# When the shared expert's weights are loaded, and in what order the expert routing is worked out, in a two-layer decoder on one core

## The reference

```python
logits = x @ w_router.T
_, top_idx = jax.lax.top_k(logits, TOP_K)            # TOP_K = 1
mask = jax.nn.one_hot(top_idx, E, dtype=logits.dtype).sum(axis=1)
scores = jax.nn.sigmoid(logits) * mask
masked_inputs = scores.T[:, :, None] * x[None, :, :]
gate_up = jnp.einsum('eth,ehf->etf', masked_inputs, gate_up_proj)
gate, up = jnp.split(gate_up, 2, axis=-1)
expert_out = jnp.einsum('etf,efh->eth', up * jax.nn.silu(gate), down_proj)
shared = jax.nn.silu(x @ w_gate.T) * (x @ w_up.T) @ w_down.T
out = shared + expert_out.sum(axis=0)
```

## Time and profile before

| | |
|---|---|
| median of three runs | 1583.07 us |
| the profiled execution | 1582.05 us |
| its span | 1580.3 us |
| PE busy | 1408.4 us (89%) |
| DVE busy | 1085.4 us (69%) |
| ACT busy | 742.1 us (47%) |
| POOL busy | 334.6 us (21%) |
| mean granted clock of PE | 0.94 of full speed |

### The profile page before, as it was taken

The page is one execution under the profiler, slowest core; times in us unless marked ns, Lnnn a source line. Parts: engine busy times, 40 slices in busy tenths (PEclk is TensorE's granted clock), DMA queues, the critical chain, the costliest instruction groups (busy, mean ns, idle before and its releaser), DMA issues. The chain is left out here.

```text
span 1580.3 us, 24782 instructions
## 1 busy us (share of the span) xinstructions
PE 1408.4 (89%) x9358; PEld 758.7 (48%) x9358; DVE 1085.4 (69%) x2384; ACT 742.1 (47%) x995; POOL 334.6 (21%) x393
## 2 busy tenths in 40 slices
PE   6876699968999979868998889999999999999976
PEld 3544478844989876422334512333333333332555
DVE  3899655542221217866984789999999999994447
ACT  2444344421111111324664315777778777778431
POOL 3323210013000017742334520000000000000241
PEclk9998899979999999858999968999999999999998
DMA  9644600025889841673430650342223422220001
GB/s 345 222 146 146 187 1 1 1 87 208 290 280 304 276 148 53 192 214 118 130 91 15 185 178 1 83 101 67 64 64 86 101 65 64 64 63 2 1 1 53
DMA packets 148745, 185.57 MB, mean 117 GB/s; under 512 B 15723, under 2 KB 124799, under 8 KB 148498
## 3 DMA queue, kind: packets, MB, share of 16 engines
q1 hardware_dynamic: 135836, 150.65, 31.7%
q0 software_dynamic: 9200, 29.64, 6.0%
q10 hardware_dynamic: 3590, 3.70, 0.7%
HBM read 129.52 MB, written 54.15 MB: 116 GB/s over the span
## 5 line engine op out<-in xcount | busy, mean ns | idle before, releaser
L1934 DVE TENSOR_REDUCE xa_part<-psum 128x1 f32<-128x512 f32 x768 | 481.6, 683 | 25.9 <-PE psum L1795 24.9
L1894 ACT ACTIVATE xa_P<-psum 128x1024 f32<-128x1024 f32 (+1 forms) x416 | 403.2, 1021 | 139.0 <-PE psum L1819 137.7
L1819 PE MATMUL psum<-sa_Q,xa_K 50*128 50x512 bf16 (+3 forms) x1664 | 262.9, 380 | 4.6 <-DMA sa_Q<-xa_mrow 3.6
L1795 PE MATMUL psum<-xa_K,sa_Q 48*128 48x512 bf16 x768 | 241.0, 397 | 6.0 <-DVE xa_part L1934 4.5
L1835 PE MATMUL psum<-xa_P,xa_V 128*32 128x512 f32 (+1 forms) x1664 | 222.5, 607 | 0.4 <-ACT xa_P L1894 0.4
L1795 PEld LDWEIGHTS psum<-xa_K,sa_Q 48*128 48x128 bf16 x768 | 59.1, 93 | 234.8 <-DVE xa_part L1934 203.5
L1931 DVE CUSTOM_DVE_ANT_0 psum<-psum,cf_sb 128x128 f32<-128x128 f32 (+3 forms) x256 | 119.5, 517 | 32.4 <-PE psum L1795 32.2
L1819 PEld LDWEIGHTS psum<-sa_Q,xa_K 50*128 50x128 bf16 (+3 forms) x1664 | 102.5, 96 | 76.9 <-ACT xa_P L1894 20.9
L1187 PEld LDWEIGHTS psum<-xtT,wgu 128*128 128x128 f32 x992 | 115.5, 192 | 5.8 <-issue 4.6
L1187 PE MATMUL psum<-xtT,wgu 128*128 128x128 f32 x992 | 115.9, 275 | 1.4 <-issue 0.8
L1894 ACT ACTIVATE sa_P<-psum 128x1024 f32<-128x1024 f32 (+3 forms) x128 | 83.5, 707 | 57.0 <-PE psum L1819 56.8
(11 more groups left out here) (241 smaller groups left out, 2170.5 us busy)
## 6 DMA issues: line engine op xcount, KB each, us to landing
wgu<-in_f_gu SPq DMA_DIRECT2D x31, 1024.0 KB, 6.2
xa_K<-kx SPq DMA_DIRECT2D x192, 100.1 KB, 5.1
wdn<-in_f_dn SPq DMA_DIRECT2D x31, 512.0 KB, 6.6
vx<-xv_v SPq DMA_DIRECT2D x48, 256.0 KB, 3.8
xa_V<-vx POOLq DMA_DIRECT2D x16, 768.0 KB, 6.5
sa_Q<-qs SPq DMA_DIRECT2D x64, 96.0 KB, 2.3
sa_K<-ks SPq DMA_DIRECT2D x64, 96.0 KB, 2.3
sa_Q<-qx SPq DMA_DIRECT2D x64, 96.0 KB, 2.3
```

The costliest lines, as they stand in the source:

```text
L1795: last = pe.matmul(out[:, 0:width], hb.q(u)[tile:tile + HALF, to, qt * P:(qt + 1) * P], hb.k(u)[tile:tile + HALF, to, e * BANK:e * BANK + ...
L1819: last = pe.matmul(out(j), hb.k(u)[tile:tile + depth, to, kt * P:kt * P + r], hb.q(u)[tile:tile + depth, to, q0(kt):L], start=(half == 0), ...
L1894: act.activation(Pr[0:r, (u * KT + kt) % PR, h:h + 2, 0:w_], S_PS(p)[0:r, :, 0:w_], ACT.Exp, scale=SCALE).then_inc(s_exp, 1)
L1934: dve.tensor_reduce(part[:, g % 2, col + qt, e:e + 1], src, AX, ALU.max).then_inc(s_1free, 1)
```

## The change

It has four parts.

1. The three loads of list "f" are issued by SP in `l0_xattn`, behind the context's loads, and no longer by ACT in `l0_ffn`. Their semaphore f_w is made there. The weights lie in a region of their own, `big_weights`, allocated for the whole program ahead of layer 0; layer 1's last weights (list "d") take the same region later.
2. On PE, the rank matmuls stand between the gate half and the up half of item 1, instead of behind item 1.
3. On DVE, the order behind the counts becomes: clearing cs, the sigmoid, item 0's product, the steps to the tile ends, the table, item 1's product, the slots; then, ahead of the products of items 2, 3, 4 and 5, four scalings each.
4. In `combine_and_prepare` the tiles of `Values` are allocated ahead of those of `Split`, and in `heads_loop` ACT gets one more wait, `keys.val.sp_end(act)`, for all stores of the values, ahead of its first exponential.

```diff
--- before.py
+++ after.py
@@ -801,6 +801,7 @@
+        env.s_fw = sem("f_w")
@@ -814,6 +815,8 @@
+                for dst, src in env.loads["f"]:
+                    sp.dma_start(dst, src).then_inc(env.s_fw, 16)
@@ -1055,20 +1057,22 @@
-        def shared_pe(pe, n):
+        def shared_pe(pe, n, halves=range(2)):
             c, f = items[n]
             if n == 0:
-                pe.wait_ge(s_fw, 16 * len(env.loads["f"]))
+                pe.wait_ge(env.s_fw, 16 * len(env.loads["f"]))
...
-            for e, name in enumerate(("f_wg", "f_wu")):
+            for e in halves:
+                name = ("f_wg", "f_wu")[e]
...
-            last.then_inc(s_sps, 1)
+            if e == 1:
+                last.then_inc(s_sps, 1)
@@ -1198,12 +1202,13 @@
-                    for n in range(2):
-                        shared_pe(pe, n)
+                    shared_pe(pe, 0)
+                    shared_pe(pe, 1, (0,))
                     pe.wait_ge(s_cnt, 1)
                     pe.matmul(PS[:, BANK:BANK + E], env.tri, pre[:, T, :], start=True, stop=True)
                     pe.matmul(PS[:, BANK + E:BANK + 2 * E], env.ones, pre[:, T, :], start=True,
                               stop=True).then_inc(s_rank, 1)
+                    shared_pe(pe, 1, (1,))
@@ -1232,8 +1237,6 @@
-                    for dst, src in env.loads["f"]:
-                        act.dma_start(dst, src).then_inc(s_fw, 16)
@@ -1293,14 +1296,11 @@
                     ins.then_inc(s_cnt, 1)
-                    shared_dve(dve, 0)
+                    link(dve.memset(cs[:, :, :], 0.0))
                     dve.wait_ge(s_ex, 1)
                     link(dve.tensor_scalar(e1[:, :], en[:, :], 1.0, None, ALU.add))
                     link(dve.reciprocal(sg[:, :], e1[:, :]))
-                    for t in range(T):
-                        dve.tensor_scalar(xs[:, t, :], env.x[:, t, :], sg[:, t:t + 1], None, ALU.mult).then_inc(s_xs, 1)
-                    shared_dve(dve, 1)
-                    link(dve.memset(cs[:, :, :], 0.0))
+                    shared_dve(dve, 0)
                     dve.wait_ge(s_rank, 1)
@@ -1311,18 +1311,21 @@
                     end = cs[:, 0, E:2 * E]
+                    link(dve.tensor_tensor(le[:, :, :], end[0:1, :].unsqueeze(1).to_broadcast([1, ETILES, E]),
+                                           iota32[0:1, :].unsqueeze(2).to_broadcast([1, ETILES, E]), ALU.is_le))
+                    link(dve.tensor_reduce(tf[:, :], le[:, :, :], AX, ALU.add))
+                    link(dve.tensor_scalar(tf2[:, :], tf[:, :], float(E - 1), None, ALU.min))
+                    dve.tensor_copy(table[:, :], tf2[:, :]).then_inc(s_tab, 1)
+                    shared_dve(dve, 1)
                     link(dve.tensor_tensor(st[:, :], end, nt[:, :], ALU.subtract))
...
                     dve.tensor_copy(slot[:, :], sf[:, :]).then_inc(s_slot, 1)
...
                     for n in range(2, ROUTE_ITEMS):
+                        for t in range((n - 2) * TB, min((n - 1) * TB, T)):
+                            dve.tensor_scalar(xs[:, t, :], env.x[:, t, :], sg[:, t:t + 1], None, ALU.mult).then_inc(s_xs, 1)
                         shared_dve(dve, n)
@@ -1381,9 +1384,9 @@
+        val = Values(env, c_, "sv", [(b, tuple(range(TB)), P) for b in range(B)], env.vs)
         sp_ = Split(env, c_, "sqk", L, bias, dst, lambda n: [(part,) for part in SLOTS[blocks[n][1]]], 4,
                     rope=lambda n: (env.cos, env.sin_neg if blocks[n][2] == 0 else env.sin))
-        val = Values(env, c_, "sv", [(b, tuple(range(TB)), P) for b in range(B)], env.vs)
@@ -1904,6 +1907,7 @@
                     act.wait_ge(keys.split.s_lo, keys.rest[-1] + 1)
+                    keys.val.sp_end(act)
@@ -2367,6 +2377,8 @@
+        big = sb("big_weights", [P, 3 * KD * F], F32)
+        weights("f", ctx, big)
@@ -2388,10 +2400,8 @@
-        with ExitStack() as c0:
-            weights("f", c0)
-            later_keys = l0_ffn(nc, env, sa)
-        weights("d", ctx)
+        later_keys = l0_ffn(nc, env, sa)
+        weights("d", ctx, big)
```

More of the change, by code:

```diff
@@ L1031, in l0_ffn @@
         s_l1 = sem("f_l1")
-        s_fw = sem("f_w")
         s_dve = sem("f_dve")
@@ L2341, in build, with weights @@
         env.w, env.loads = {}, {"a": [], "c": [], "f": [], "1": [], "d": []}
-        def weights(layer, c):
+        def weights(layer, c, region=None):
             sbw, _ = alloc(c)
+            used = 0
             for name, (k, n, l) in MATS.items():
@@ L2351, in weights @@
                     else:
-                        t = sbw(name + "_sb", [P, k // P, n], F32)
+                        if region is None:
+                            t = sbw(name + "_sb", [P, k // P, n], F32)
+                        else:
+                            t = region[:, used:used + k // P * n].rearrange("p (k n) -> p k n", n=n)
+                            used += k // P * n
                         env.w[name] = t
```

## The result

| | before | after |
|---|---|---|
| median | 1582.88 us (8 runs, 1574.33 to 1587.16) | 1568.84 us (8 runs, 1562.37 to 1574.76) |
| the profiled execution | 1582.05 us | 1574.76 us |
| its span | 1580.3 us | 1573.0 us |

The ratio is 0.991, with a 95% interval of 0.9889 to 0.9932. The sign and what bounds the block were right; three terms of the sum were not. Three executions in all the measurements (1831.3, 2025.97 and 3388.97 us) were far slower than the rest and count in no median or ratio here.

The account below looks back on a forecast made before the run. Bound: TensorE's expert tiles, started late by the shared items and scatters behind late weights. First turn 10.8 us sooner, less 2.0 for the clock, gives 8.8: 1573.25 us profiled, forecast 1574.3; range 1569.8 to 1579.5.

Parts of the forecast that it names:

- what bounds the block: Feed-forward block: TensorE-bound expert tiles from 386.5 to 577 us; whatever starts them sooner is passed on whole.
- the sum: Whole kernel: 10.8 us gained at the first turn, less 2.0 for the clock, 8.8 us.
- both chains: Ahead of the expert tiles: ten shared items and the scatters end last at about the same time; both must move.
- the load costs nothing: SP's queue in the stage before: SP has nothing else to issue, engines move 1 GB/s; 135 us to spare.
- the new wait is covered: Layer 1 self attention: ACT's 2.9 to 4.0 us delay fits in PE's 5.93 us idle time, 1.9 us to spare.
- the lock: DVE scalings beside POOL scatters: the engines hold each other up; 2.0 us taken, between nothing and 4.3.
- the clock: PE behind the first turn: after idling some 4 us it starts at the lower clock, costing 2.0 us.
- the landing: Last scatter to row loads: kept as before, within the 25.03 us from first scatter to first turn.
- rival 2: Scatters and items: the lock costs in full, 2.8 us for the clock; 5.2 gained, 1577.9 us; chance 0.14.
- rival 1: Scatters: the lock costs nothing, slots at 346.5; 13.3 us gained less 1.65, 1571.4 us; chance 0.16.

Follow-up runs that it names:

- the kernel with the wait later: Changed kernel with ScalarE's new wait moved behind the first four exponentials of the heads: median 1570.14 us, ratio 0.9919 to before.
- the burst of 16: Changed kernel with all 16 scalings straight behind the slots instead of four ahead of each of four products: median 1569.1 us, ratio 0.9895 to before.
- layout only: Kernel before with only the new allocations and ACT's new wait, old load place and orders: median 1582.75 us, ratio 0.9975.
- loads only: Changed kernel with DVE's and PE's orders of before, keeping the early loads and their allocations: median 1572.09 us, ratio 0.993 to before.
- the late rank: Changed kernel with the rank matmuls behind the whole of item 1 again: median 1571.24 us, ratio 0.9913 to before.
- the eleventh item: Changed kernel with eleven instead of ten shared items ahead of the expert tiles: median 1566.99 us, ratio 0.9907 to before.

## Why the prediction was right, and where it was too small

**Right: what bounds the block, and that both chains move.** PE waits neither for weights nor for hT, and the last thing to be late is the chain of scatters. The first turn was forecast at 374.7 with a block start at 332.54, that is +42.2; the profile has +38.9.

**Right: the load costs nothing.** SP issued the three loads at 200.2 to 201.6 us, and the stage that they run in (from its first matmul to the feed-forward block) took 148.0 and 150.5 us in the change's two profiles, 148.2 and 150.6 in before's.

**Right: the new wait is covered**, to a tenth of a microsecond against before (+33.8 against +33.9) and to 0.4 against the kernel with the wait later, and its delay of 4.1 us was within 0.1 of the upper bound.

**Wrong in size: the sum.** Six terms, counted from the block's start, in microseconds gained against the prediction:

| term | predicted | measured | gained |
|---|---|---|---|
| slots ready | +14.46 | +14.02 | 0.44 |
| slots to first scatter | 0.64 | 1.11 | -0.47 |
| first to last scatter, with the lock | 19.31 + 2.0 | 19.19 | 2.12 |
| last scatter to row loads | 3.69, as before | 2.41 | 1.28 |
| row loads to turn | 2.03 | 2.16 | -0.13 |
| the clock behind the turn | 2.0 | 0 (1.6 in the second profile) | 2.0 |

Their sum is 5.2 us, and 8.8 + 5.2 = 14.0. What failed are three terms that were sized too high: the lock (2.0, measured 0), the landing (3.69, measured 2.41) and the clock (2.0, measured 0 or 1.6). Each is a step of the text:

- "I take 2.0" for the lock. The two engines do hold each other up: the rows at 613 pointed to it, and the burst of 16 shows it. What failed is the step from one blocked instruction to a price for sixteen. I let each burst hit POOL; in fact the first burst is over when the first scatter starts, and beside the second and third it is one scaling of DVE's that waits, 0.1 to 0.2 us each, while the scatters keep their pace. The rule of the Trainium skill (SBUF — State Buffer, Who interferes with whom) is that whoever starts first keeps the pair for the whole instruction and the other blocks. The trace agrees with it only in part: the scatter in the burst of 16 waits, and a scaling that reaches the end of a scatter waits for that end, but scalings that began up to 0.45 us into a scatter ran at their usual 0.34 us. The rule names no total; the order of the two engines' instructions had to be walked through one by one, and rival 2 was priced without that.
- "As before" for the landing. I let the 25.03 us from first scatter to turn stand, as if the DMA engines were as full as before. In before the table came last, so the first experts' 4.5 MB were still moving when the last scatter was issued; with the table first they are done by then. The windows from the last scatter to the row loads, in before and then in after (DMA share and GB/s are the last two numbers):

```profile
379.80:383.50 3.70, 3.70 (x10) 1.55 (x9) 0.69 (x1) 0.60 (x1) 0.93 (x1) 1.00 0.61 228
```

```profile
375.10:377.50 2.40, 2.40 (x7) 0.94 (x5) 0.64 (x1) 0.00 (x0) 0.93 (x1) 1.00 0.31 109
```

  The experiments divide cleanly by this: with the table last (before twice, layout only, loads only) it is 3.7 to 4.6 us, with the table first (all the others, the one with the late rank and the one with the burst among them) 2.4. That the moving weights are the reason is read from the windows; no run changes the traffic alone. "The 18 us by which the table comes sooner are worth nothing by themselves" was therefore wrong by 1.3 us.
- "I take 2.0" for the clock. I reckoned with 4 us of idling; it was 1.8, since the turn came 3.3 us sooner than thought. The price was about right where the clock does fall (1.6 to 2.5 us). It did so in one of the change's two profiles, so how much of this term the medians hold is not known.

**The range.** All three errors were in one direction, and rival 1, which had the lock at nothing, kept the other two terms. Its 1571.4 with 1.3 us less for the landing and 1.65 less for the clock would have been 1568.4. The low end had 1.6 us beyond rival 1, not enough for the landing and the clock together.

**What stays open.** The total moved by 14.0 us in the medians, as much as the turn did. That the first stages add nothing is the likeliest reading of fourteen block starts that lie between 332.4 and 340.8 us with either layout; a difference of 1 or 2 us in their mean can't be excluded with these runs. The stages behind the first gather took 984 to 993 us in these profiles, so they too hide such a difference. Open as well: what delays ACT's silu ahead of the turn in some executions, and what lets the clock fall behind one stop of 1.8 us and not behind another.

## What to carry to other kernels

Where the parts of a change lie on one chain, they add up at the end of that chain: 10.9 and 3.0 us apart, 14.1 together. Read them there; further on, one fall of the clock (2.8 us in the loads-only profile) looks like an interaction. Moving a step that starts large loads ahead of a stream of small DMAs can shorten the landing of the stream's last transfer, even if nobody waits for those loads: 2.4 us here instead of 3.7. And when an engine idles for a transfer right ahead of a long run of matmuls, work from the run itself can fill the gap: the eleventh item gave 1.7 us at the first gather for one changed number.

## What the runs showed of the hardware

- VectorE and GpSimd hold each other up, and who waits depends on the moment. A DMA_INDIRECT that began 1.2 us into 16 back-to-back scalings took 3.21 us instead of 1.10 and ended 0.12 us behind the last of them; the 16 took the same 4.29 us as with GpSimd idle. Beside shorter bursts only the end of a DMA_INDIRECT of 0.96 us holds VectorE up: scalings that began up to 0.45 us into it took their usual 0.34 us, those that began 0.51 to 0.72 us into it ended 0.09 us behind its end. One that began 0.08 us into a burst of four took its usual 0.96 us.
- The first scatter starts 0.3 us behind the slots if its data has long been there, and 1.1 us behind them (0.85 us behind the end of the first scaling) if the scalings come after the slots.
- A stop of 1.8 us let the granted clock fall to 0.50 in one execution and not in another of the same program, and the 32 matmuls behind it took 5.44 or 3.81 us. Over all kernels it fell behind stops of 1.75, 1.90, 2.15 and 2.36 us and not behind 1.82 and 2.38. Behind a stop of 5.27 us the 32 matmuls took 5.90, and without one 3.81.
- The same instructions of the first two stages took 332.4 to 340.8 us in fourteen profiled executions. A single profile's span is no measure of a change of 1%. Counted from the stage's own start the first turn repeats to 1.3 us, and the stretch of expert tiles behind it to 0.01 us (202.92 or 202.93) in seven profiles in which the clock stays up.
